# Selective scan on one core: the inflows that TensorE makes come for two states at a time in 64x128 tiles, and dt*u moves from GpSimd to VectorE

## The reference, cut to what matters

```python
u = jax.nn.silu(u)                                        # 256 channels
dbc = u @ xproj_w.T
dt = jax.nn.softplus(dbc[..., :dt_rank] @ dt_w.T + dt_b)
Bm = dbc[..., dt_rank:dt_rank + d_state]                  # 16 states
Cm = dbc[..., dt_rank + d_state:]
dA = jnp.exp(dt[..., None] * A)
dBu = (dt * u)[..., None] * Bm[:, :, None, :]
def step(h, inp):
    dA_t, dBu_t, C_t = inp
    h = dA_t * h + dBu_t
    return (h, jnp.einsum('bdn,bn->bd', h, C_t))
```

## Time and profile before

| | |
|---|---|
| median of 3 runs | 1566.91 us (1558.56 to 1570.34) |
| the profiled execution, its own time | 1558.44 us |
| its span, first to last instruction | 1556.6 us |
| mean granted TensorE clock | 0.975 of full speed |
| busy in the span: TensorE matmul, VectorE, GpSimd, ScalarE | 1347.9, 1161.2, 1060.3, 958.4 us |

### The profile page before, as it was taken

One profiled execution on the slowest core, in us unless ns is written; L12 is line 12 of the kernel. 1 busy time (PEld: TensorE's weight loads), 2 busy tenths in 40 slices (PEclk: granted clock), 3 DMA queues, 4 the chain that ended last, 5 costly groups with the idle time before them and its releaser, 6 DMA issues.

```text
span 1556.6 us, 43543 instructions
## 1 busy us (share of the span) xinstructions
PE 1347.9 (87%) x17914; PEld 1014.4 (65%) x17914; DVE 1161.2 (75%) x1926; ACT 958.4 (62%) x1750; POOL 1060.3 (68%) x684
## 2 busy tenths in 40 slices
PE   6798888889889989889889777898998999997595
PEld 3566766656756666666666666457997666666594
DVE  6788888888898887888888886523335888876376
ACT  6877777777766776876876765313555555542144
POOL 3798888888898888888888886340333466583552
PEclk9899999999999999999999989999999999999798
DMA  5122232232232222222222220531124200001223
GB/s 189 58 93 95 85 107 81 85 108 80 85 103 80 91 102 80 91 102 80 95 98 79 97 91 29 213 98 36 52 79 126 98 1 2 2 29 54 80 64 98
DMA packets 51604, 128.95 MB, mean 83 GB/s; under 512 B 8080, under 2 KB 33168, under 8 KB 41696
## 3 DMA queue, kind: packets, MB, share of 16 engines
q1 hardware_dynamic: 46640, 116.36, 21.8%
q0 software_dynamic: 4768, 9.81, 1.9%
HBM read 113.20 MB, written 18.56 MB: 85 GB/s over the span
## 4 chain that ended last, share of the span: by engine, by line
PE 52%; ACT 15%; DVE 15%; issue 8%; POOL 5%; another core or an unknown queue 2%; DMA 1%; SPq 1%; DVEq 0%; ACTq 0%; POOLq 0%
PE py L530 8%; PE pa L508 8%; DVE hh L925 5%; ACT da L723 4%; POOL hc L1077 3%; PE pr L1990 2%; PE bank L1536 2%; PE bank L1532 2%; PE bank L1546 2%; PE pq L413 2%; PE pq L385 2%; PE pr L2004 2%; ACT uz L625 2%; DVE hh L902 2%; PE pr L2193 2%
## 5 line engine op out<-in xcount | busy, mean ns | idle before, releaser
L1077 POOL TENSOR_TENSOR hc<-hh,cs 128x1024 f32<-128x1024 f32 x256 | 602.9, 2363 | 138.5 <-DVE hh L925 70.6
L925 DVE TENSOR_TENSOR_SCAN hh<-da,st,pa 128x512 f32<-128x512 f32 x240 | 293.6, 1266 | 65.5 <-PE pa L508 55.5
L508 PEld LDWEIGHTS pa<-dg,dtut 64*64 64x64 f32 x10240 | 180.8, 137 | 179.4 <-issue 175.6
L530 PE MATMUL py<-ident,hc 128*128 128x128 f32 x2048 | 277.1, 279 | 19.3 <-ACT yt L743 19.2
L508 PE MATMUL pa<-dg,dtut 64*64 64x64 f32 x10240 | 219.1, 226 | 80.9 <-DVE yz L934 38.5
L530 PEld LDWEIGHTS py<-ident,hc 128*128 128x128 f32 x2048 | 227.8, 142 | 44.7 <-ACT yt L743 21.2
L723 ACT ACTIVATE da<-dt,w 128x512 f32<-128x512 f32 x320 | 212.7, 711 | 11.3 <-DVE hh L925 10.4
L723 ACT ACTIVATE pa<-dt,w 128x512 f32<-128x512 f32 x192 | 127.7, 684 | 97.2 <-DVE hh L925 96.4
L925 DVE TENSOR_TENSOR_SCAN hh<-pa,st,hh 128x512 f32<-128x512 f32 x144 | 175.4, 1267 | 2.6 <-ACT pa L723 1.9
L385 PE MATMUL pq<-xn,w 128*128 128x512 f32 x248 | 121.0, 613 | 5.0 <-ACT xn L759 3.6
L925 DVE TENSOR_TENSOR_SCAN hh<-da,pa 128x512 f32<-128x512 f32 x80 | 93.2, 1207 | 29.4 <-PE pa L508 26.3
(11 more groups left out here) (349 smaller groups left out, 2807.8 us busy)
## 6 DMA issues: line engine op xcount, KB each, us to landing
cs<-bcrows SPq DMA_DIRECT2D x64, 1024.0 KB, 4.7
bs<-bcrows SPq DMA_DIRECT2D x32, 256.0 KB, 3.9
xsorted<-in_pads SPq DMA_DIRECT2D x13, 387.0 KB, 5.3
rot<-in_rot SPq DMA_DIRECT2D x4, 1024.0 KB, 5.0
wx<-in_l_w SPq DMA_DIRECT2D x4, 1024.0 KB, 10.3
ysort<-ytoken SPq DMA_DIRECT2D x14, 256.0 KB
wx<-in_l_w SPq DMA_DIRECT2D x1, 3072.0 KB, 12.3
wx<-in_l_w SPq DMA_DIRECT2D x1, 2304.0 KB, 16.7
```

The costliest lines, as they stand in the source:

```text
L508: i = pe.matmul(pa[turn["step", s, h] % SLOTS][c * HQ:(c + 1) * HQ, kt * P + r * HQ:kt * P + (r + 1) * HQ], dtut[rows, kt, h * P + c * HQ: ...
L530: i = pe.matmul(py[:, h * CH + kt * P:h * CH + (kt + 1) * P], hc[s % HCS][:, h, t], ident[:, :], is_transpose=True, start=n == 0 and kt == ...
L925: v.tensor_tensor_scan(hh[s % HHS][:, h, :], a, b, 0.0 if first else st[:, m % 2, n, h:h + 1], ALU.mult, ALU.add).then_inc(s_taken, 1)
L1077: g.tensor_tensor(hc[s % HCS][:, :, :], hh[s % HHS][:, :, :], cs[j % 2][:, s % CG, :].unsqueeze(1).broadcast_to([P, HF, CH]), ALU.mult).th ...
```

## The change

BY_G is gone: TensorE makes the inflow of twelve states (0 to 5, 8 to 11, 14, 15), VectorE of four (6, 7, 12, 13). The pairs of states that share a `dg` are always neighbours and fill two steps together. In the first step of a pair TensorE makes half h = 0 of both states, in the second half h = 1. One call of `inflow` is 8 matmuls with a weight of 64x128 and a moving operand of 64x128 (64 tokens, two states), alternating between the two row halves of the array, each of which writes a bank of its own; there is no phase 1. The results of the two states are interleaved in the two banks, so the scan reads its inflow with a stride of two elements over both. The tokens are dealt out by fours (`by_fours`), so the matmul writes its bank with a stride of eight elements. Both banks of a step come free only when both scans are done (`free`). The decays of a step of TensorE's are those of one half for two states, the C product waits for the second step of a pair for either state (`scanned`), and ScalarE keeps the states one step later.

dt*u is made by VectorE after the scan of step 13, in two halves (`dt_times_u`), each with an increment of its semaphore. GpSimd has only the diagonals and the C products left, and the DMAs of `bs` are gone.

```diff
-BY_G = (0, 12)
-BY_V = (1, 6, 11, 13)
-BY_P = tuple(n for n in range(NS) if n not in BY_G + BY_V)
+BY_V = (6, 7, 12, 13)
+BY_P = tuple(n for n in range(NS) if n not in BY_V)
...
-SLOTS = 4
+SLOTS, DAS = 4, 4
...
+                def free(i):
+
+                    i -= SLOTS
+                    return i // 2 * 2 + 2 if handed_items[i][0] == "flow" else i + 1
...
+                    return (turn["flow", pair_of(s), HF - 1, BY_P.index(k) % 2] if k in BY_P else turn["step", s, HF - 1]) + 1
...
-                    def inflow(s, phase):
-
-                        m, k = s // NS, before(BY_P, s)
-                        pair, of = k // len(BY_P) * len(PAIRS) + k % len(BY_P) // 2, k % len(BY_P) % 2
-                        if phase == 0:
-                            pe.wait_ge(s_turnk, turned_count(m, 2))
-                            pe.wait_ge(s_dg, pair + 1)
-                            if turn["step", s, HF - 1] >= SLOTS:
-                                pe.wait_ge(s_taken, turn["step", s, HF - 1] - SLOTS + 1)
-                        else:
-                            pe.wait_ge(s_pin, 2 * k + 1)
+                    def inflow(s):
+
+                        m, k, h = s // NS, pair_of(s), BY_P.index(s % NS) % 2
+                        i = turn["flow", k, h, 0]
+                        pe.wait_ge(s_turnk, turned_count(m, 2))
+                        pe.wait_ge(s_dg, k + 1)
+                        if i >= SLOTS:
+                            pe.wait_ge(s_taken, free(i + 1))
                         for kt in range(4):
                             for r in range(2):
-                                h, rows = (r + phase) % 2, slice(r * HQ, (r + 1) * HQ)
-                                for c in range(2):
-                                    i = pe.matmul(pa[turn["step", s, h] % SLOTS][c * HQ:(c + 1) * HQ, kt * P + r * HQ:kt * P + (r + 1) * HQ],
-                                                  dtut[rows, kt, h * P + c * HQ:h * P + (c + 1) * HQ], dg[pair % DGS][rows, of, kt, :],
-                                                  start=True, stop=True)
-                        i.then_inc(s_pin, 1)
+                                rows = slice(r * HQ, (r + 1) * HQ)
+                                mm = pe.matmul(pa[i % SLOTS + r].rearrange("p (j k n) -> p k n j", n=2, k=4)[:, kt, :, :],
+                                               dtut[rows, kt, h * P:(h + 1) * P], dg[k % DGS][rows, :, kt, :], start=True, stop=True)
+                        mm.then_inc(s_pin, 1)
...
+                        if s + 1 < STEPS and by_pe(s + 1) and n != 10:
+                            inflow(s + 1)
+                        if s + 2 < STEPS and by_vector(s + 2):
+                            spread_b(s + 2)
...
                         prep(m + 1, n)
+                        if n == 10:
+                            inflow(s + 1)
...
+                                inflows = pa2[i // 2 % (SLOTS // 2)][:, j::2]
+                                v.tensor_tensor_scan(hh[(NS * m + nj) % HHS][:, h, :], da[q % DAS][:, :], inflows,
+                                                     0.0 if first else st[:, m % 2, nj, h:h + 1], ALU.mult, ALU.add).then_inc(s_taken, 1)
...
+                            if n == 13:
+                                dt_times_u(m)
...
+                        for h in range(HF):
+                            v.tensor_tensor(dtu[m % 2][:, h, :], dt[m % 2][:, h, :], uz[m % 2][:, h, :], ALU.mult).then_inc(s_dtu, 1)
...
-                        if n == 13 and m + 1 < UNITS:
-                            dt_times_u(m + 1)
-                        if s + 2 < STEPS and (s + 2) % NS in BY_G:
-                            inflow(s + 2)
```

174 lines of the change are left out of this document (77 added, 97 removed).

## The result

| | before | changed | |
|---|---|---|---|
| median of the runs side by side | 1563.87 us (4) | 1661.78 us (4) | ratio 1.0615, 95% interval 1.0553 to 1.0677 |
| span of the profiled execution | 1556.6 us | 1658.2 us | +101.6 |
| last chunk of the Mamba layer kept | at 972.62 us | at 1065.57 us | +92.95 |
| mean unit (finish to finish, the last 14) | 57.98 us | 63.93 us | +5.94 |
| granted clock of TensorE, mean | 0.975 | 0.941 | |

The change costs 6%, 98 us; I had forecast +29 for the profiled execution and a range up to 1632.

What follows compares the result with a forecast made beforehand. No single engine but a chain changing engines was taken as the bound; stretches sum to +1.95 us a unit, +28 in all, plus +1.1 at the layer's end: 1587 us profiled, 1592 as median, range 1552 to 1632.

Steps and rivals of the forecast that it cites:

- it costs nothing there: After finish, VectorE's dt*u (2 x 0.67 us) is done before TensorE turns it; without cover, up to 1.3 us.
- a): Stretch from finish to the end of z's projection, 12.14 us before: forecast +0.3 us a unit.
- b): Stretch from z's projection to the scan of step 4, 10.57 us before: forecast -0.6 us a unit.
- c): Stretch from the scan of step 4 over step 5 and gate to TensorE's next start, 8.12 us before: forecast 0.
- d): Stretch from TensorE's start after gate to the end of its output projection, 14.81 us before: forecast +1.1 us a unit.
- e): Stretch from output projection over factors, two scans and finish to TensorE's start, 12.25 us before: forecast +1.15 us a unit.
- the change of shape: Each place where TensorE's array changes its tile shape costs about 0.13 us; one fewer in the first stretch.
- The end of the layer: After the last scan, two C products where there was one: forecast +1.1 us.
- The cheap change of shape: Rival, chance 0.16: inflow call takes 0.88 us, shape changes cost no 0.13; 1543 us, or about 1551 for a median.
- Nothing measurable: Rival, chance 0.12: ScalarE's mid_part after gate is not late, 1.1 us less a unit; 1572 us, within 1%.
- The clock: Rival, chance 0.14: TensorE's waits between steps 4 and 7 lower its clock in each unit, +34 us; 1626 us.
- Taking turns, and a cost of the stride: Rival, chance 0.06: tiles take turns (1.9 us a call) or strides cost; +127 us, about 1715 us.

Runs made afterwards that it cites:

- e1: Changed kernel with dt*u made by GpSimd again, in two halves: 1618.27 us, ratio 1.033 to the kernel before.
- e2: Kernel before with only dt*u moved to VectorE, in two halves after the scan of step 13: 1585.13 us, ratio 1.0129.
- e4: Changed kernel with GpSimd's C product of step 13 waiting until VectorE has made dt*u: 1617.36 us, ratio 1.0313 to the kernel before.
- e3: e4 with TensorE kept busy over its wait for the scans of step 6 by three matmuls of zeros: 1614.13 us, ratio 1.0287.
- e5: e4 with ScalarE's mid_part put ahead of the decays of step 6: 1582.43 us, ratio 1.0358 to the kernel before.
- e6: e4 with the two D*u sums tied to states 10 and 11, not 11 and 12: 1587.45 us, ratio 1.0384 to the kernel before.
- e7: e4 with VectorE's inflow of state 12 made for one column of 512 only (results wrong): 1576.27 us, ratio 1.0305 to the kernel before.
- e15: Kernel before with the pairs in 64x128 tiles alone, old places and dt*u on GpSimd: 1507.43 us, ratio 0.9864.

## Why the prediction was wrong

**The step that failed first: "it costs nothing there", said of dt*u.** I took 2 x 0.67 us from the gate's row and let TensorE cover it. The duration is right for VectorE alone (662 ns at least) and wrong beside GpSimd, up to 3.92 us for the pair, and the cover is gone in the long units. This is 2.31 us a unit, some 32 us of the layer (changed against e1), shown by e1, e2 and e4, of the 4.0 us by which the unit (63.93) is longer than forecast (57.98 + 1.95). I had bounded this cost by a tenth less and by its full 1.3, both from rows with GpSimd out of the picture.

**Stretches, in a unit without the lock.** One of e4's 60.7 us units, from TensorE's inflow at 336.50 on, cut as before; the rows at the cuts:

```profile
336.50 1.16 PE L521 MATMUL pa<-dg,dtut 64*128 64x128 f32 x16 [1.01 <-DVE dt L895]
...
349.11 1.16 PE L521 MATMUL pa<-dg,dtut 64*128 64x128 f32 x16
...
352.31 1.28 ACT L633 ACT_TABLE_LOAD   x1 [1.19 <-PE py L542]
...
357.65 4.79 DVE L938 TENSOR_TENSOR_SCAN hh<-da,st,pa 128x512 f32<-128x512 f32 x4 [1.67 <-ACT da L732]
...
366.76 1.44 DVE L954 TENSOR_TENSOR yz<-uz,pa 128x512 f32<-128x512 f32 x2
...
386.43 1.30 DVE L884 SCALAR_TENSOR_TENSOR dt<-pa,ab 128x512 f32<-128x512 f32 x2 [1.37 <-ACT pa L675]
...
395.82 1.26 DVE L895 SCALAR_TENSOR_TENSOR dt<-pa,dt 128x512 f32<-128x512 f32 x2
397.22 1.16 PE L521 MATMUL pa<-dg,dtut 64*128 64x128 f32 x16 [1.01 <-DVE dt L895]
```

- a) 12.61 us against 12.14: +0.47 (forecast +0.3).
- b) to the scan of step 4 at 357.65 + 2.4: 10.94, +0.37 (forecast -0.6). This missed by 1 us. I counted TensorE's calls, but the stretch now ends with ScalarE: the silu waits for the sum of state 12, which stands behind the inflow of state 1, and the scans of 3 and 4 wait for the decays behind the silu.
- c) 8.25: +0.13 (forecast 0).
- d) 15.6: +0.8 (forecast +1.1). TensorE starts 5.2 us after gate (forecast 5.45).
- e) 13.3: +1.0 (forecast +1.15). First factor to the end of finish: 10.65 us (forecast 10.7).

Together +2.8 in the best units, against +1.95. The mean of e4's units is 61.38, another 0.65 a unit: units of 62 and 64 us stand among those of 60.7. Some 0.5 of it is the clock, which lengthens d by 1.5 to 2.9 us in four units (see e3). The sum by stretches saw one path; e5, e6 and e7 took something off it and got nothing or 0.16 us back, which fits paths beside it that are as long.

**The mechanism of c to e was right in kind**: states 6 and 7 on VectorE make TensorE wait by over 2 us for the scans of step 6, state 12 lengthens the way from factor to finish. But for all of the change except dt*u I had +1.95 a unit, and it is 4.30 + 0.67 - 1.33 = +3.64. By my own prices the pairs were to bring 0.2 us for each of ten states and 0.13 for the change of shape, 2.1 together, which leaves 4.1 for places and load. They brought 1.33 where they were tried alone, and places and load cost 4.97: both terms missed by 0.8 to 0.9 us. A call of 1.09 us and not 1.05 is part of the first.

**The end of the layer** (last finish to last chunk) was +1.1 in the forecast, +9.2 in the changed kernel and +3.2 in e4; I did not follow it further.

**Two readings in the prediction.** The 0.89 us that it reads as eight transposes is L526, eight plain matmuls; eight transposes with no 64x64 group near take 0.94 (424.10 to 425.04), so a change of shape costs 0.08 there and not 0.13, which moves the sum by 0.05. The floor of 25 ns between starts, which it names under Part 3, stands in Part 1 of that page of the Trainium skill; Part 3 has the tiles of a packed group start about 4 ns apart. In the trace of the kernel before, neighbouring starts in a group of 64x64 tiles are 6 to 7 ns apart, which is near that. The sum went by the row and does not rest on either figure.

**The rivals.** The cheap change of shape: a call is 1.09 us, so not by its mechanism, yet the pairs alone do make the kernel faster (e15). Nothing measurable: ScalarE was late as counted, and e5, which takes that lateness out, gains nothing. The clock: partly. It falls in the long units (0.90) and in many short ones (0.97), against my 1.00, and costs some 13 us of the layer in the changed kernel and 8 in e4 in the stretch read at e3, not 34; what it costs elsewhere was not read. Taking turns, and a cost of the stride: no. None of the rivals was the lock, and the range ended 30 us short.

## What to carry to other kernels

Before an elementwise instruction moves from GpSimd to VectorE, look where its operands lie and what GpSimd runs at that time: two operands in SBUF beside GpSimd's products, which read SBUF too, made 1.3 us into 3.8 here, and it depends on who starts first, so the same code has short and long units. Test a change of several parts by whole parts, each put alone on the kernel before: here one of four (the pairs) gave 1.4% and the other three took it back more than fivefold. What a part is worth depends on what it is added to (0.5 to 3.3 us a unit for the pairs), so a single order of steps is not its price. And when load is moved between engines, look at the busy share of each in the stretch where it lands, not in the whole unit: before the change VectorE was busy in 49.5 of 57.9 us of a unit, but in 13.65 of the 14.65 us where state 7 was put.
